# Grouped convolution and attention-weighted mixing on one core: whole-row transfers for the first unit, and another order of the first stage

## The reference

```
# L0: x = x + conv(x) + ctx
out = lax.conv_general_dilated(x, weight, window_strides=(1,), padding=[(4, 4)], feature_group_count=4)
ctx = jnp.einsum('nd,od->no', c, c_weight)
out = out + ctx[:, :, None] + bias[None, :, None]
# L1: x = x + mix(x)
h = jax.nn.gelu(embedding @ W0 + b0, approximate=False)
h = jax.nn.gelu(h @ W1 + b1, approximate=False)
att = jax.nn.softmax((h @ W2 + b2) / T, axis=-1)
agg_w = jnp.einsum('bk,koi->boi', att, weight[..., 0])
agg_b = att @ bias_k
out = jnp.einsum('boi,bih->boh', agg_w, x) + agg_b[:, :, None]
```

## Time and profile before

| | us |
|---|---|
| median of three runs | 253.8 |
| the profiled execution | 254.94 |
| its span, first to last instruction | 253.1 |
| PE busy | 238.5 (94%) |
| DVE busy | 224.2 (89%) |
| ACT busy | 88.1 (35%) |
| POOL busy | 27.1 (11%) |
| DMA, mean over the span | 272 GB/s |

### The profile page before, as it was taken

How to read it: one execution, slowest core, us unless ns; L and a number is a source line. 1 busy time by engine, 2 the same in 40 slices (tenths; PEclk the granted TensorE clock), 3 DMA queues, 4 the chain that set the end, 5 groups by cost and what they waited for, 6 DMA issues and landing times.

```text
span 253.1 us, 5772 instructions
## 1 busy us (share of the span) xinstructions
PE 238.5 (94%) x2164; PEld 95.1 (38%) x2164; DVE 224.2 (89%) x148; ACT 88.1 (35%) x142; POOL 27.1 (11%) x52
## 2 busy tenths in 40 slices
PE   7379999999999999999999999999999999999970
PEld 5253233333333333333333343444443444444720
DVE  0531899999999999999999999999999999999690
ACT  2305253331423333333405142333333253222370
POOL 1021421010101010010101010101001010101000
PEclk9679999999999999999999999999999999999998
DMA  6999593999999999898979899999999896444456
GB/s 162 253 280 277 136 206 63 331 231 409 332 368 250 394 224 385 245 361 289 330 272 276 340 257 370 243 390 216 362 276 342 273 301 254 166 166 168 166 233 267
DMA packets 29483, 68.72 MB, mean 272 GB/s; under 512 B 3281, under 2 KB 5585, under 8 KB 29473
## 3 DMA queue, kind: packets, MB, share of 16 engines
q1 hardware_dynamic: 19536, 51.41, 61.5%
q10 hardware_dynamic: 9936, 17.17, 25.6%
HBM read 35.02 MB, written 33.55 MB: 271 GB/s over the span
## 4 chain that ended last, share of the span: by engine, by line
PE 89%; DMA 3%; DVE 3%; POOL 1%; ACT 1%; ACTq 0%; issue 0%; POOLq 0%
PE yps L494 63%; PE zps L517 20%; DMA zout<-in_mix_w 3%; DVE ynat L459 2%; PE zps L476 2%; PE yps L564 1%; PE yps L533 1%; DVE ycol L454 1%; PE zps L544 1%; PE zps L582 0%; ACT L325 0%; ACTq L321 0%; DVE xin L465 0%; POOL wraw L256 0%; POOL zout L252 0%
## 5 line engine op out<-in xcount | busy, mean ns | idle before, releaser
L494 PE MATMUL yps<-xph,wraw 64*64 64x512 f32 x1488 | 167.1, 590 | 0.3 <-DVE xph L387 0.3
L299 ACT ACTIVATE zout<-zps,gamu 128x512 f32<-128x512 f32 x120 | 72.7, 689 | 132.7 <-PE zps L517 89.8
L494 PEld LDWEIGHTS yps<-xph,wraw 64*64 64x64 f32 x1488 | 59.7, 132 | 100.4 <-issue 100.0
L395 DVE STREAM_TRANSPOSE ycol<-yps 128x1024 f32<-128x1024 f32 x62 | 74.5, 1220 | 9.1 <-PE yps L494 8.4
L387 DVE STREAM_TRANSPOSE xph<-xin 128x2112 f32<-128x2112 f32 x32 | 74.8, 2339 | 2.2 <-DMA xin<-in_x 2.2
L405 DVE STREAM_TRANSPOSE ynat<-ycol 128x2048 f32<-128x2048 f32 x30 | 67.6, 2290 | 1.1
L517 PE MATMUL zps<-ynat,mixv 64*64 64x512 f32 x480 | 57.3, 589 | 0.0
L235 POOL COPY mixv<-mixt 128x512 f32 (+1 forms) x16 | 17.5, 1094 | 179.0 <-ACT zout L299 174.5
L517 PEld LDWEIGHTS zps<-ynat,mixv 64*64 64x64 f32 x480 | 20.1, 132 | 31.0 <-issue 30.5
L307 ACT ACTIVATE mixt<-zps 128x1024 f32<-128x1024 f32 x8 | 7.8, 1021 | 16.9 <-PE zps L476 16.9
L564 PE MATMUL yps<-zout 128*128 128x256 f32 x20 | 8.3, 593 | 2.0 <-POOL zout L241 1.3
(11 more groups left out here) (51 smaller groups left out, 30.3 us busy)
## 6 DMA issues: line engine op xcount, KB each, us to landing
out<-zout SPq DMA_DIRECT2D x60, 512.0 KB, 5.0
xin<-in_x SPq DMA_DIRECT2D x60, 258.0 KB, 7.1
xin<-in_x ACTq DMA_DIRECT2D x60, 258.0 KB, 7.4
out<-xin SPq DMA_DIRECT2D x4, 512.0 KB, 4.9
xin<-in_x ACTq DMA_DIRECT2D x4, 132.0 KB, 4.7
xin<-in_x SPq DMA_DIRECT2D x4, 130.0 KB, 4.7
xin<-in_x SPq DMA_DIRECT2D x4, 128.0 KB, 6.1
xin<-in_x ACTq DMA_DIRECT2D x4, 126.0 KB, 5.9
```

The source lines that it names most:

```text
L299: nc.scalar.activation(zout[:, o].rearrange("p (i c j q) -> p c i j q", i=2, c=2, q=PH)[:, c], zps[:, at:at + BANK].rearrange("p (q i j) - ...
L395: nc.vector.transpose(ycol[:, :, :, :, :, g].rearrange("p i s j q c -> p (i s j) q c"), yps[:, 2 * BANK * (g % 2):2 * BANK * (g % 2) + 2 * ...
L494: last = nc.tensor.matmul(yps[C * c:C * c + C, at:at + BANK].rearrange("p (s f) -> p s f", s=S // 2), wsum[rows, b, g], xph[slot][c][rows, ...
```

## The change

Three things are changed, all in the first stage. First, x of unit 0 is loaded like that of any other unit, in eight transfers of whole rows, and both transposes wait for all of it; `x_first` is gone. With that, `shares` goes to the front of ACT's DMA queue, and `mixw` is issued by ACT behind the warm-up activation and no longer behind the exponential. Second, the first aggregation stands in front of the convolution and no longer inside its first group, with `keep_on` before it and after it, and the others move up by a group; ACT's queue and VectorE's queue are written in an order that goes with it. Third, the mask of the shares is four activations on ScalarE (one for each set, scaled by a column of `turn`) in place of one VectorE instruction.

```
-            for k in range(KQ):
-                for t in range(2):
-                    sp.dma_start(*x_piece(0, 0, 0, k, t, 0)).then_inc(x_first, 16)
-            sp.dma_start(shares[:], share).then_inc(share_in, 16)
-            for k in range(KQ):
-                for t in range(2):
-                    sp.dma_start(*x_piece(0, 0, 0, k, t, 1)).then_inc(x_in[0], 16)
+            load(0, 0)
...
+            act.dma_start(shares[:], share).then_inc(share_in, 16)
+            load(0, 0)
             act.wait_ge(zeroed, 1)
             nc.scalar.activation(warm[:], warm[:], ACT.Gelu)
-            for t in range(2):
-                act.dma_start(*x_piece(0, 0, 1, 0, t, 1)).then_inc(x_in[0], 16)
+            act.dma_start(mixw, mix_w).then_inc(mix_in, 16)
...
             load(1, 1)
+            act.wait_ge(share_in, 16)
+            act.wait_ge(mm, 4)
+            for o in range(RO):
+                nc.scalar.activation(attt[:, o], sps[:, 0:NS], ACT.Copy, scale=turn[:, o:o + 1]).then_inc(soft, 1)
             gather(0, 0)
             gather(0, 1)
+            load(2, 0)
             gather(1, 0)
...
             phases(0, 0, 0)
-            dve.wait_ge(mm, 4)
-            nc.vector.tensor_tensor(attt, sps[:, 0:NS].unsqueeze(1).broadcast_to([P, RO, NS]),
-                                    turn.unsqueeze(2).broadcast_to([P, RO, NS]), ALU.mult).then_inc(soft, 1)
             phases(0, 0, 1)
...
-                pe.wait_ge(soft, 4)
+                pe.wait_ge(soft, 7)
                 pe.wait_ge(beta_made, 2)
                 pe.wait_ge(mix_eye, 1)
-                pe.wait_ge(w_sum, 1)
                 aggregate(0)
...
+            keep_on(4)
             pe.wait_ge(share_in, 16)
             pe.wait_ge(soft, 3)
             nc.tensor.matmul(sps[:, 0:NS], att[:].rearrange("p o e -> p (o e)"), eye,
                              start=True, stop=True).then_inc(mm, 1)
+            keep_on(6)
+            first_aggregate()
             pe.wait_ge(turned, 1)
-            keep_on(6)
+            keep_on(4)
             pe.wait_ge(w_in, 16)
-            conv(0, 0, 0, (first_aggregate,))
-            conv(0, 0, 1, (second_aggregate,))
-            conv(0, 0, 2, (output_constants, None, third_aggregate))
-            conv(0, 0, 3, (None, None, fourth_aggregate))
-            conv(1, 1, 0, (None, None, pair_constants))
-            conv(1, 1, 1)
+            pe.wait_ge(w_sum, 1)
+            conv(0, 0, 0, (second_aggregate,))
+            conv(0, 0, 1, (third_aggregate,))
+            conv(0, 0, 2, (fourth_aggregate,))
+            conv(0, 0, 3, (output_constants,))
+            conv(1, 1, 0)
+            conv(1, 1, 1, (None, None, pair_constants))
```

44 lines of the change are left out of this document (14 added, 30 removed).

## The result

| | before | changed |
|---|---|---|
| median, us | 253.84 (253.37 to 253.95, 4 runs) | 255.88 (255.33 to 257.6, 4 runs) |
| ratio, 95% interval | | 1.0087 [1.0059, 1.0115] |
| profiled execution, us | 254.94 | 255.85 |
| its span | 253.1 | 254.1 |

The change is slower by 0.9%, and 255.88 lies outside the predicted range of 252.1 to 254.6. Measured once more beside other kernels it was slower by less (1.0036 [1.0013, 1.006]).

What follows compares the result with a forecast made beforehand. VectorE, idle-free after conv group 3 of unit 0, was taken to bound the kernel. Paths of 16.95, 16.95 and 17.1 gave T about 17.2, gain 18.0 - T = 0.8 us: 254.1 profiled, 253.0 median; range 252.1 to 254.6.

Steps and rivals of the forecast that it cites:

- What bounds: Whole kernel: VectorE, without idle time since 33.31, counts; TensorE is within 0.1 us of it.
- that point: End of conv group 3 of unit 0, at 33.24 us before; the end of the kernel was to move equally.
- Rival 4: TensorE bounds after all and the first mixing counts: gain 1.1 us larger, 251.9 us; chance 0.08.
- T: Start of the convolution after the change, the latest of three paths: about 17.2 us; gain 18.0 - T.
- (a): TensorE's own queue before the convolution: zero products, aggregation 1.07, four zero products 1.75, giving T = 16.95.
- (b): x of unit 0: lands at 12.2, both transposes behind it, T = landing + 4.74 = 16.95.
- the sum: TensorE's pieces from T to the end of group 3: conv instructions, three aggregations and constants, 15.22 us.
- break-even landing of 13.3: Landing time of unit 0's x from which rival 2 decides, giving T = 18.0.
- Rival 2: x of unit 0 is late with both transposes behind it; landing at 14.3 gives T = 19.0, 254.8 us; chance 0.14.
- rival 1: TensorE's clock comes back only at 15.3, not 11.9: T = 18.5, 0.5 us lost, 254.3 us; chance 0.15.
- (c): `mixw` path: lands at 14.0, first addition 0.3, then 1.07 + 1.75, giving T = 17.1.
- Rival 3: New wait on reordered queues: third `gather` late or unit 1's x behind 25.1; 253.3 to 254.0 us; chance 0.06.

Runs made afterwards that it cites:

- e_no_gap: Changed kernel with nine zero products, not six, ahead of the first aggregation and six behind it that wait for nothing; 254.91 us, ratio 1.0066.
- e_quiet: Changed kernel with conv weights, constants, `mixw` and unit 1's x issued only once unit 0's x has landed; 259.43 us profiled, one run.
- e_free_whole: e_front_whole without the hold on unit 1's x, four zero products behind the first aggregation, unit 1's first part turned between groups 0 and 1; 254.24 us, 1.0027.
- e_after_hold: Changed kernel with unit 1's x issued only once unit 0's x has landed; 255.12 us, ratio 1.005.
- e_hold_warm: e_hold with four more zero products behind the small network and twelve behind the turned shares, none waiting for the first transpose; 253.69 us, ratio 1.0004.
- e_hold: Kernel before with `mixw` issued behind the warm-up activation and unit 1's x issued only once unit 0's has landed; 253.11 us, ratio 0.9964.
- e_cut_rows: Changed kernel with x of unit 0 in two cuts per row again, the first transpose waiting for the first cuts only; 253.87 us, ratio 1.0019.
- e_cut_no_gap: e_cut_rows with nine zero products ahead of the front aggregation and two behind it that wait for nothing; 255.08 us, ratio 1.0032.
- e_front: e_hold with the first aggregation ahead of the convolution, the others a group earlier, the fourth behind group 3; 254.07 us, ratio 1.001.
- e_front_whole: e_front with x of unit 0 in whole rows and the mask ahead of both transposes; 255.41 us, ratio 1.0049.
- e_cut_hold: Changed kernel with cut rows, unit 1's x held until unit 0's landed, zero products that wait for nothing, fourth aggregation still in group 2; 255.14 us, 1.0056.
- e_free: e_front without the hold on unit 1's x, four zero products behind the first aggregation, unit 1's first part turned between groups 0 and 1; 253.22 us, 0.9968.
- e_whole_only: Kernel before with only whole rows for x of unit 0 and `shares` at the front of ACT's queue; 256.53 us, ratio 1.0111.

## Why the prediction was wrong

**What bounds: right.** "The end moves by as much as that point moves": 2.21 us at group 3, 2.21 at the last unit, and 219.1 us behind turn in 16 profiles. The reading of the earlier trace rows over the chain of the earlier trace rows held. Rival 4 is out: the end moved by as much as group 3, and the front aggregation was worth nothing where the fourth took its place (16.80 against 16.81 from T to turn).

**The failed step is the latest of (a) and (b), T = 17.2; T was 19.67.** From T to the emptying of group 3 the sum had 15.22; at full clock it is 15.52 (e_no_gap, 17.88 to 33.40), an error of 0.3: the first conv instructions take 1.01 (17.88 to 18.89 there) and not 0.86, the rest is hand-over between pieces. The miss of 3.0 us at group 3 (35.52 against about 32.5) is then made of these:

- *(b), x lands at 12.2.* It landed at 14.01, and T behind it is 18.7: 1.5 late. The rate was better than I took (293 GB/s against 277), the bytes were not: 0.191 x 8 + 0.293 x 5.9 is 3.26 MB by then, and I had let only 0.13 MB of others pass ahead of the last piece. It was 0.8 MB. The later transfers on both queues were served beside the earlier ones. The sum also gave x a rate that only the full queues show: alone (e_quiet) it drew 192 GB/s. How much of the 1.8 us the passing bytes cost is not shown, since profiles with about 0.55 MB of others ahead have x at 12.81 and 12.86. Seven profiles of whole rows without anything held, or with only unit 1 held, have 14.01, 13.83, 13.93, 12.96, 12.91, 12.86 and 12.81, and e_free_whole 12.65; even with empty queues it is 12.50. My 12.2 lay below all of them, the break-even landing of 13.3 amid them, with three of nine beyond it. All four on one chip lie from 12.50 to 12.86, but on another the same queues gave 13.83 and 12.96, so the chip alone is not the reason. Rival 2 named this mechanism and its price, T = landing + 4.74 (17.80 for 12.91 in e_after_hold is 4.89), at a chance of 0.14, small for three of nine.
- *(a), "aggregation 1.07, four zero products 1.75".* I priced (a) and (b) as paths side by side. They are one: the wait for `turned` stands ahead of the four zero products, so they start when the first transpose ends, at 16.44, and have only the second's 2.26 to hide in. At full clock that is enough. At half clock they take 3.30: 1.0 late. The first conv records at 1.41 instead of 1.09 add 0.3.
- *The clock, rival 1.* I asked when it comes back. It had not gone: the granted clock was 1.00 from 8 to 14.3 and 0.99 to 17, with four more zero products behind the small network (e_hold_warm against e_hold, which differ in such products and their wait alone, has 1.00 against 0.70 from 8 to 14). They do not always hold it: the same four took 2.83 to 3.78 us in place of 1.99 in e_cut_rows, e_cut_no_gap, e_front, e_front_whole, e_cut_hold and e_free. It fell later, after gaps of 1.72 (for `mixw`) and 0.55 (for the transpose), which I had not looked for, in some executions and not in others.
- *(c), `mixw`.* Additions at 14.35, aggregation at 14.75, predicted 14.0 and 14.3: right within 0.5. But it opened the gap.

Hidden, as predicted: the mask on ScalarE, unit 1's transposes, and the issues for unit 2. The latter began at 18.68 and ended at 21.47, and TensorE waited for no copy. Rival 3 is out.

In the Trainium skill, "TensorE: Matmul & The Clock Gate", section "What's actually happening", the stretch over which activity is judged is said not to restart with the kernel, so that the clock's changes shift from run to run. The two profiles of the same changed kernel agree with it, as far as two can: zero products behind the aggregation at 3.30 in one profile and 1.99 in the other, although the idle ahead of the aggregation was the longer in the second. By the Trainium skill, "DMA: Bandwidth & Descriptors", section "Specifications", full rate is reached at 512 B a row, so that rows of 1 KB lose nothing; from 8 to 14.3 us the longer rows moved 293 GB/s against 239, with other loads beside them too, so no run isolates the row. The higher rate brought the last landing from 14.29 only to 14.01.

What stays open: what decides in one execution whether the clock falls, why the products behind the small network took up to twice their time in six profiles and ran at full speed in the others, what moves the landing of x between 12.65 and 14.01, what slowed most runs of e_no_gap, and whether e_hold's 0.7 us come from the hold.

## What to carry to other kernels

The load that was first in its queue did not land after its own bytes (3.0 to 3.3 MB had moved, where 2.46 were its own and those ahead): take the account with what is queued behind it, and prefer a cut whose first part releases work, since that work hides the scatter of the second. When an instruction is moved in front, look for what takes its place in the stretch that counts; the fourth aggregation in group 2 gave back exactly the first. Filler products that keep the clock up should wait for nothing that is on the path (5.49 us in e_whole_only, 3.30 here), and their price at half clock, not at full, is what must fit behind the cover.

## What the runs showed of the hardware

- The granted clock's record and the length of a product can part. In e_free the record says 1.00 from 8 to 14 us, yet each zero record took 0.47 us from 8.56 on and 0.25 at 16.63; e_front_whole shows the same. That it was the clock is read from the length, which is that of half clock elsewhere (0.46 in e_whole_only, where the record says 0.50). The length is what costs time, so read it beside the record:

```profile
8.00:14.00 6.00, 6.00 (x17) 4.96 (x18) 3.37 (x4) 1.30 (x4) 1.48 (x5) 1.00 1.11 268
```

- The last four stores of 512 KB land in 3.6 us or in 4.9 to 5.0, nothing between, in 17 and in 3 of 20 profiles. It moves the time of an execution by 1.3 us, about as much as the profiled run of before stood above its median (1.14).
- x of one unit in whole rows landed anywhere from 12.65 to 14.01 in eight profiles with much the same transfers queued (12.96 and 13.83 with the same queues on the same chip), an amount as large as the effects that the prediction weighed against each other.
